# Gated cross-attention and feed-forward block, 8 batches on one core: the last batch in two halves of 112 queries, and a new order of all steps

## The reference, cut to what matters

```python
for b in range(8):                       # x: 8 x 224 x 512, ctx: 8 x 750 x 512, all float32
    q = layer_norm(layernorm(x[b])) * gq + betq ; c = layer_norm(ctx[b]) * gkv + betkv
    Q, K, V = q @ Wq + bq, c @ Wk + bk, c @ Wv + bv          # 16 heads of 32
    o = softmax(Q_h @ K_h.T / sqrt(32)) @ V_h                # per head: 224 x 750
    x1 = x[b] + tanh(g_x) * (concat_h(o) @ Wo + bo)
    h  = relu(layernorm(x1) @ ternary(W1).T + b1)            # 224 x 2048
    out[b] = x1 + tanh(g_f) * (h @ ternary(W2).T + b2)
```

## Time and profile before

| | us |
|---|---|
| median of 3 runs | 966.37 (963.3 to 967.71) |
| profiled execution, its own time | 963.93 |
| its span, first to last instruction | 962.1 |
| TensorE busy | 901.3 (94%) |
| VectorE busy | 745.5 (77%) |
| ScalarE busy | 641.4 (67%) |
| GpSimd busy | 298.2 (31%) |

### The profile page before, as it was taken

The page is one execution under the profiler, slowest core; times in us unless marked ns, Lnnn a source line. Parts: engine busy times, 40 slices in busy tenths (PEclk is TensorE's granted clock), DMA queues, the critical chain, the costliest instruction groups (busy, mean ns, idle before and its releaser), DMA issues.

```text
span 962.1 us, 22304 instructions
## 1 busy us (share of the span) xinstructions
PE 901.3 (94%) x8868; PEld 686.9 (71%) x8868; DVE 745.5 (77%) x1378; ACT 641.4 (67%) x1330; POOL 298.2 (31%) x517
## 2 busy tenths in 40 slices
...
GB/s 283 185 206 237 140 130 133 192 149 1 82 64 175 2 2 111 54 157 1 33 96 191 2 3 127 84 110 1 64 33 139 1 4 62 154 17 2 42 1 20
DMA packets 52039, 84.03 MB, mean 87 GB/s; under 512 B 6392, under 2 KB 33528, under 8 KB 50936
## 3 DMA queue, kind: packets, MB, share of 16 engines
...
## 4 chain that ended last, share of the span: by engine, by line
PE 78%; DVE 9%; DMA 5%; ACT 4%; SPq 3%; issue 1%; POOL 0%; DVEq 0%; ACTq 0%; POOLq 0%
PE ps_fill L481 49%; PE ps_pv L528 8%; PE ps_score L496 7%; PE ps_exp L512 7%; PE ps_fill L538 4%; DMA ctx_raw<-ctx_in 3%; DVE row_max L786 2%; SPq L401 2%; DVE p_parts L794 1%; PE ps_fill L586 1%; DVE bn L826 1%; DMA h_parts<-w2t 1%; ACT ps_exp L665 1%; ACT p_parts L664 1%; DVE h_parts L975 1%
## 5 line engine op out<-in xcount | busy, mean ns | idle before, releaser
L786 DVE TENSOR_REDUCE row_max<-ps_score 128x1 f32<-128x750 f32 x256 | 238.1, 930 | 34.7 <-PE ps_score L496 33.4
L794 DVE TENSOR_TENSOR p_parts<-ps_exp,p_parts 125x448 f16<-125x448 f32 x384 | 233.2, 617 | 33.8 <-ACT ps_exp L665 31.6
L664 ACT ACTIVATE p_parts<-ps_exp 125x448 f16<-125x448 f32 x384 | 209.1, 544 | 68.6 <-PE ps_exp L512 51.3
L665 ACT ACTIVATE ps_exp<-ps_exp 125x448 f32<-125x448 f32 x384 | 211.0, 549 | 0.0
L496 PE MATMUL ps_score<-k_stack,q_stack 96*128 96x375 f16 x512 | 128.1, 332 | 12.4 <-DVE row_max L786 11.9
L512 PE MATMUL ps_exp<-q_stack,k_stack 100*125 100x224 f16 x768 | 128.9, 267 | 7.3 <-DVE p_parts L794 5.6
L528 PE MATMUL ps_pv<-v_now,p_parts 125*128 125x66 f16 x3072 | 115.7, 194 | 2.8 <-DVE o_sum L802 1.3
L528 PEld LDWEIGHTS ps_pv<-v_now,p_parts 125*128 125x128 f16 x3072 | 109.3, 98 | 11.9 <-issue 3.5
L481 PE MATMUL ps_fill<-w_ternary,h_parts 128*128 128x256 fp8e4 x1024 | 116.6, 273 | 0.0
L512 PEld LDWEIGHTS ps_exp<-q_stack,k_stack 100*125 100x125 f16 x768 | 89.0, 139 | 29.0 <-DVE p_parts L794 6.9
L481 PEld LDWEIGHTS ps_fill<-w_ternary,h_parts 128*128 128x128 f16 x1024 | 99.4, 98 | 13.9 <-DVE ctx_t_lo L871 0.9
(11 more groups left out here) (139 smaller groups left out, 1550.5 us busy)
## 6 DMA issues: line engine op xcount, KB each, us to landing
...
```

The source lines that it names most:

```text
L664: nc.scalar.activation(ph[0:KR, unit, :], ps_exp[0:KR, u, 0:2 * NQ], ACT.Exp, scale=EXP_SCALE)
L665: nc.scalar.activation(ps_exp[0:KR, u, 0:2 * NQ], ps_exp[0:KR, u, 0:2 * NQ], ACT.Exp, scale=EXP_SCALE).then_inc(exp_done, 1)
L786: nc.vector.tensor_reduce(mx[:, i // 2, i % 2:i % 2 + 1], ps_score[:, :, 0:KH], AX.XY, ALU.max) \
L794: nc.vector.tensor_tensor(pl[0:KR, unit, :], ps_exp[0:KR, u, 0:2 * NQ], ph[0:KR, unit, :], ALU.subtract).then_inc(p_split, 1)
```

## The change

The attention and feed-forward of batch 7 are regrouped. `score`, `expo`, `pv`, `mr`, `split`, `f1` keep their number of steps, but a step of batch 7 now belongs to one half of 112 queries: scores 0 to 15 are the 16 heads of half 0, scores 16 to 31 those of half 1; `expo.3h` to `expo.3h+2` and `pv.h` take two heads of one half (h below 8: half 0); `f1.0` to `f1.3` are the 16 chunks of half 0, `f1.4` to `f1.7` those of half 1. An `expo` has four matmuls of 112 moving columns instead of two of 224, with the same 125 stationary columns each; a `pv` still has 24 matmuls of 66 moving columns, but 112 stationary ones instead of 128; an `f1` has 32 matmuls of 112 columns instead of 16 of 224, and ScalarE lifts it in four pieces of 112 instead of two of 224. `ot`, `op`, `yt`, `f2`, `score` work on 112 queries instead of 128. `divide`, `rstd2`, `bias2` and `store` of batch 7 become two steps, one per half, and their waits are per half. Nothing is computed twice or left out in either kernel.

Then the tail of half 0 up to `yt.0@7` is put in the list ahead of `pv.15@7`, and `f1.0@7` to `f1.3@7` right behind it, between the steps of half 1.

All three lists are new: they hold the same steps, but also in `OPENING` and `ROUND` nearly every step stands elsewhere. `OPENING` now reaches a little further, to `pv.15@1`. On SyncE's queue the end is now `kq.0@7 vc.0@7 vc.1@7 kq.1@7 kq.2@7 store.0@5 kq.3@7 vc.2@7 vc.3@7 xb.0@6 store.0@6 xb.0@7 store.0@7 store.1@7`.

After the change TensorE's queue ends `pv.11@7 f2.3@6 expo.39@7 pv.12@7 ot.0@7 expo.40@7 mr.7@7 expo.41@7 expo.42@7 expo.43@7 expo.44@7 pv.13@7 op.0@7 expo.45@7 expo.46@7 pv.14@7 expo.47@7 yt.0@7 pv.15@7 f1.0@7 f1.1@7 f1.2@7 ot.1@7 f1.3@7 op.1@7 f2.0@7 f2.1@7 yt.1@7 f1.4@7 f1.5@7 f1.6@7 f1.7@7 f2.2@7 f2.3@7`, and VectorE's `f2_add.3@6 max.31@7 part.39@7 part.40@7 ot_lo.0@7 part.41@7 part.42@7 take.12@7 part.43@7 part.44@7 take.13@7 op_add.0@7 rstd2.0@7 part.45@7 take.14@7 part.46@7 part.47@7 yt_lo.0@7 take.15@7 f1_hi.0@7 divide.1@7 ot_lo.1@7 f1_hi.1@7 f1_hi.2@7 f1_hi.3@7 op_add.1@7 rstd2.1@7 f2_add.0@7 f2_add.1@7 yt_lo.1@7 ...`.

```diff
@@ ENDING, last lines @@
-    f1_hi.7@6 pv.14@7 part.37@7 part.38@7 take.11@7 part.39@7 max.31@7 part.40@7 f2_add.0@6 take.12@7 f2.3@6
-    f2_add.1@6 part.41@7 take.13@7 part.42@7 split.7@7 part.43@7 pv.15@7 part.44@7 part.45@7 part.46@7 part.47@7
-    f2_add.2@6 f2_add.3@6 take.14@7 take.15@7 divide.0@7 bias.0@7 ot.0@7 ot.1@7 norm2.0@7 ot_lo.0@7 norm2.1@7 op.0@7
...
+    f2.3@6 max.28@7 take.9@7 f2_add.0@6 part.31@7 expo.39@7 pv.12@7 part.32@7 max.29@7 f2_add.1@6 part.33@7 max.30@7
+    part.34@7 part.35@7 take.10@7 divide.0@7 ot.0@7 expo.40@7 mr.7@7 expo.41@7 expo.42@7 part.36@7 part.37@7
+    take.11@7 expo.43@7 part.38@7 f2_add.2@6 expo.44@7 pv.13@7 f2_add.3@6 max.31@7 bias.0@7 op.0@7 part.39@7
+    part.40@7 ot_lo.0@7 part.41@7 part.42@7 take.12@7 part.43@7 part.44@7 take.13@7 expo.45@7 op_add.0@7 expo.46@7
+    pv.14@7 expo.47@7 norm2.0@7 yt.0@7 rstd2.0@7 part.45@7 take.14@7 part.46@7 part.47@7 pv.15@7 f1.0@7 yt_lo.0@7
+    take.15@7 f1_hi.0@7 divide.1@7 f1.1@7 f1.2@7 ot.1@7 ot_lo.1@7 f1_hi.1@7 f1.3@7 op.1@7 f2.0@7 norm2.1@7 f2.1@7
+    f1_hi.2@7 bias2.0@7 yt.1@7 f1.4@7 f1_hi.3@7 op_add.1@7 rstd2.1@7 f1.5@7 f1.6@7 f1.7@7 f2_add.0@7 f2_add.1@7
+    yt_lo.1@7 f1_hi.4@7 f1_hi.5@7 f1_hi.6@7 f2.2@7 f2.3@7 f1_hi.7@7 f2_add.2@7 bias2.1@7 store.1@7 f2_add.3@7
 
+        LAST = B - 1
+        HQ = NQ // 2
+
+        def half(t):
+
...
+                    if n == LAST:
+                        for t in range(2):
+                            sp.dma_start(xb[0:HQ, t, :], x[n][half(t), :]).then_inc(xb_loaded, 16)
+                    else:
+                        load_rows(n, xb, xb_loaded)
                 elif kind == "kq":
                     copy_kq(i, n)
                 elif kind == "vc":
                     copy_v(i, n)
+                elif kind == "store" and n == LAST:
+                    sp.wait_ge(out_ready, n * 4 + 2 * i + 2)
+                    sp.dma_start(out[n][half(i), :], xb[0:HQ, i, :]).then_inc(out_stored, 16)
                 elif kind == "store":
                     sp.wait_ge(out_ready, n * 4 + 4)
...
                     pe.wait_ge(kq_landed[h // 4], n * 96 + 96)
                 if n == 0 and i == 0:
                     pe.wait_ge(bias_row_ready, 3)
                 else:
                     pe.wait_ge(max_taken, n * 32 + i)
-                for half in range(2):
-                    last = pe.matmul(ps_score[:, half, 0:KH],
-                                     q_stack[0:SPLIT_ROWS, h, QSTART[t]:QSTART[t] + P],
-                                     k_stack[0:SPLIT_ROWS, h, half * KH:half * KH + KH],
-                                     start=True, stop=True)
+                q = half(t) if n == LAST else slice(QSTART[t], QSTART[t] + P)
+                for s in range(2):
+                    last = pe.matmul(ps_score[0:q.stop - q.start, s, 0:KH], q_stack[0:SPLIT_ROWS, h, q],
+                                     k_stack[0:SPLIT_ROWS, h, s * KH:s * KH + KH], start=True, stop=True)
                 last.then_inc(scores_ready, 1)
 
...
                     pe.wait_ge(p_split, n * 48 + (i - 2))
-                for kt in (2 * u, 2 * u + 1):
-                    last = pe.matmul(ps_exp[0:KR, u, (kt % 2) * NQ:(kt % 2) * NQ + NQ],
-                                     k_stack[0:STACK_ROWS, h, kt * KR:kt * KR + KR],
-                                     q_stack[0:STACK_ROWS, h, :], start=True, stop=True)
+                if n == LAST:
+                    for c in range(4 * u, 4 * u + 4):
+                        hc, kt = 2 * (h % 8) + c // KT, c % KT
+                        last = pe.matmul(ps_exp[0:KR, u, (c % 4) * HQ:(c % 4 + 1) * HQ],
+                                         k_stack[0:STACK_ROWS, hc, kt * KR:kt * KR + KR],
+                                         q_stack[0:STACK_ROWS, hc, half(h // 8)], start=True, stop=True)
+                else:
+                    for kt in (2 * u, 2 * u + 1):
+                        last = pe.matmul(ps_exp[0:KR, u, (kt % 2) * NQ:(kt % 2) * NQ + NQ],
+                                         k_stack[0:STACK_ROWS, h, kt * KR:kt * KR + KR],
+                                         q_stack[0:STACK_ROWS, h, :], start=True, stop=True)
                 last.then_inc(logits_ready, 1)
 
             def pv(h, n):
 
-                if h % 4 == 0:
+                if n == LAST:
+                    if h % 2 == 0:
+                        pe.wait_ge(v_landed[h % 8 // 2], n * 32 + 32)
+                elif h % 4 == 0:
                     pe.wait_ge(v_landed[h // 4], n * 32 + 32)
                 pe.wait_ge(p_split, n * 48 + (3 * h + 3))
                 if n * 16 + h >= 1:
                     pe.wait_ge(o_taken, n * 16 + h)
+                if n == LAST:
+                    for c in range(2 * KT):
+                        for part in (ph, pl):
+                            last = pe.matmul(
+                                ps_pv[0:HQ, c // KT * 2 * VW:(c // KT + 1) * 2 * VW],
+                                part[0:KR, 3 * (h % 2) + c // 4, (c % 4) * HQ:(c % 4 + 1) * HQ],
+                                v_now[0:KR, c % KT, 2 * (h % 8) + c // KT].rearrange("p a b -> p (a b)"),
+                                start=(c % KT == 0 and part is ph), stop=(c % KT == KT - 1 and part is pl))
+                    last.then_inc(pv_done, 1)
+                    return
                 for t in range(2):
                     for kt in range(KT):
...
                                  lambda a, c: whl["o"][a][:, c, :])
                 elif kind == "yt":
                     pe.wait_ge(y_normed, n * 2 + (i + 1))
-                    last = turn(P, bank, yo[:, i, :])
+                    rows = HQ if n == LAST else P
+                    last = turn(rows, bank, yo[:, i, :], rows)
                 elif kind == "f1":
+                    if n == LAST:
+                        if i % 4 == 0:
+                            pe.wait_ge(y_split, n * 2 + i // 4 + 1)
+                        for j in range(4):
+                            m = slice((i % 4 * 4 + j) * P, (i % 4 * 4 + j + 1) * P)
+                            last = three(ps_fill[:, bank, j * HQ:(j + 1) * HQ], lambda a, c: w1q[:, c, m],
+                                         lambda a, c: o_t[a][:, c, half(i // 4)], order=((0, 0), (0, 1)))
+                        last.then_inc(fill_ready, 1)
+                        return
                     if i == 0:
                         pe.wait_ge(y_split, n * 2 + 2)
...
 
-                        if c % 2 == 0:
+                        if n == LAST:
+                            if c % 4 == 0:
+                                pe.wait_ge(h_split, n * 8 + 2 * i + c // 4 + 1)
+                        elif c % 2 == 0:
                             pe.wait_ge(h_split, n * 8 + (c // 2 + 1))
                     t, w = i // 2, slice((i % 2) * 256, (i % 2 + 1) * 256)
-                    r = slice(QSTART[t], QSTART[t] + P)
-                    last = three(ps_fill[:, bank, 0:256], lambda a, c: (hh, hl)[a][:, c, r],
+                    r = half(t) if n == LAST else slice(QSTART[t], QSTART[t] + P)
+                    last = three(ps_fill[0:r.stop - r.start, bank, 0:256], lambda a, c: (hh, hl)[a][:, c, r],
                                  lambda a, c: w2q[:, c, w], order=((0, 0), (1, 0)), chunks=FC,
-                                 ready=ready if i == 0 else None)
+                                 ready=ready if i == 0 or (n == LAST and i == 2) else None)
                 last.then_inc(fill_ready, 1)
 
...
                 dve.wait_ge(scores_ready, n * 32 + (i + 1))
+                if n == LAST:
+                    h, t = i % H, i // H
+                    if i % 4 == 0:
+                        dve.wait_ge(max_split, (n - 1) * 8 + (h // 2 + 2))
+                    nc.vector.tensor_reduce(mx[0:HQ, h, t:t + 1], ps_score[0:HQ, :, 0:KH], AX.XY, ALU.max) \
+                        .then_inc(max_taken, 1)
+                    return
                 if i % 4 == 0 and n:
                     dve.wait_ge(max_split, (n - 1) * 8 + (i // 4 + 1))
...
+                                            ps_pv[0:HQ, 0:4 * VW].rearrange("p (h s d) -> p h d s", h=2, s=2),
+                                            AX.X, ALU.add).then_inc(o_taken, 1)
+                    return
                 nc.vector.tensor_reduce(o_sum[:, :, h, :],
                                         ps_pv[:, 0:4 * VW].rearrange("p (t s d) -> p t d s", t=2, s=2),
                                         AX.X, ALU.add).then_inc(o_taken, 1)
+
+            def divide_half(t, n):
+
+                dve.wait_ge(o_taken, n * 16 + 8 * t + 8)
+                nc.vector.reciprocal(rden[0:HQ, t, :], o_sum[0:HQ, t, :, HD]).then_inc(o_recip, 1)
+                dve.wait_ge(o_recip, n + (t + 1))
+                dve.wait_ge(y_split, n * 2)
+                nc.vector.tensor_tensor(yo[0:HQ, t, :].rearrange("p (h d) -> p h d", h=H),
+                                        o_sum[0:HQ, t, :, 0:HD],
```

(8 more changed lines are left out.)

366 lines of the change are left out of this document (219 added, 147 removed).

## The result

The changed kernel takes 973.98 us (median of 4 runs, 972.99 to 976.52), the kernel before 965.89 us (4 runs): ratio 1.009, 95% interval 1.0058 to 1.0121. It is slower; 958 was forecast, at most 968. The profiled execution took 972.99 us with a span of 971.2.

A forecast was written before the change was run, and what follows sets the result against it. TensorE was taken to bound the rounds and, after the change, batch 7's attention. Tail -14.6, attention +6.4, rounds and opening 0 gave -8.2 us: 955.7 profiled, median 958, 8-in-10 range 946 to 968.

The forecast's parts named there:

- part 1: Tail behind `pv.15@7`: overlapping the halves takes it from 53.1 to 38.5 us, minus 14.6.
- the sum without clock: Tail behind `pv.15@7`: its steps added at full clock, 36.3 us, before 2.2 was added for the clock.
- parts 2 and 3: Last `pv` of batch 6 to that of 7: moved steps add 4.3 us to TensorE, narrower loads 7.7 and 1.9.
- the sum by pieces: Last `pv` of batch 6 to that of 7, kernel before: TensorE's work at full clock, one piece per kind, 64.8 us.
- Waiting: of 10.5 us much was VectorE's, which now has more cover ... 6.5 in all: Last `pv` of batch 6 to that of 7: TensorE's waits go from 10.5 to 6.5 us, 3 of them new.
- Half clock: 6.0 before, the cause of most of it gone: 2.5: Last `pv` of batch 6 to that of 7: half-clock cost, laid to the wait for batch 7's V, falls to 2.5 us.
- 0 to 1 us: At `score.12@7`: wait for the copies of `kq.3@7` behind `store.0@5`, 0 to 1 us, counted within the waiting.
- Part 4: New order of the rest: rounds minus 0.9 and plus 0.9 us; opening 0, with 4 us either way.
- Minus 0.9 and plus 0.9: Rounds: the long one may lose its 0.9 us, and a possible new TensorE wait in each adds 0.9.
- the rounds pay: Rival: K, Q or V copies asked for too late at each batch change, 3.7 to 10 us, so 966; chance 0.13.
- 4 more: Last `pv` of batch 6 to that of 7: 4 us above the forecast 87.7 if waits stay at 10.5.
- dearer loads: Rival: narrow loads hold TensorE's array as long as `expo`'s pace allows, plus 13.7 us, so 980; chance 0.08.

The follow-up runs named there:

- warm_end: Changed kernel plus 64 idle matmuls, results overwritten, where TensorE waited near the start and end of batch 7's attention; 967.94 us, 1.0000 to 1.0041 against the kernel before.
- wide_pv: Changed kernel with `pv` of batch 7 loading 128 columns of p again instead of 112; 966.86 us, 0.9963 to 1.0012 against the kernel before.
- narrow_all: Kernel before with every `pv` product except the first head's loading 112 columns of p instead of 128; 1026.33 us, 1.0563 to 1.0624 against the kernel before.
- full_new_lists: Kernel before, full tiles and its own tail, with the changed kernel's `OPENING` and `ROUND`; 972.11 us, 1.0013 to 1.0062 against the kernel before.
- kq_first: Changed kernel with batch 7's last key and value copies ahead of batch 5's store on SyncE; 973.68 us, 1.0035 to 1.0094 against the kernel before.
- warm_keys: Changed kernel with 64 idle matmuls where TensorE waited and batch 7's last key and value copies ahead of batch 5's store; 968.91 us, 1.0017 to 1.0066 against before.
- early_half: Changed kernel with half 0's steps up to `yt.0` between `pv.9` and `pv.13`, its residual in a free buffer, batch 6's f2 between last heads; 971.62 us.

## Why the prediction was wrong

- **The tail (part 1): right.** 38.5 forecast, 37.9 measured; in warm_end, at the full clock, 35.9 against the 36.3 of the sum without clock. The gap at `yt.1` is there, the clock is 1 from a few us on. The 15 us are the halves' overlap, of which some 2 are clock.
- **TensorE's work in the stretch (parts 2 and 3): the total right, in part by luck.** Loads of 112 columns at 133 ns, `pv` 1.22 (1.2 forecast), `expo` 0.22 to 0.25 (0.23); in all 79.0 us against 78.7. But the windows have TensorE busy 74.00 us in the kernel before, so 74.0 - 6.0 = 68.0 at the full clock where the sum by pieces had 64.8, and the halves added 79.0 - 68.0 = 11.0 and not 13.9. The two errors cancel. wide_pv and narrow_all show that the width of the loads alone costs 7 to 8 us; without it the changed kernel would be level with the one before (0.9963 to 1.0012).
- **The failed step: "Waiting: of 10.5 us much was VectorE's, which now has more cover ... 6.5 in all" and "Half clock: 6.0 before, the cause of most of it gone: 2.5".** The waits were 12.5 and the half clock 7.4, together 10.9 us more than the 9.0 put down. Four things were wrong in it. The base: 10.5 was the remainder of a sum that was 3.2 us short, and TensorE stood idle 81.30 - 74.00 = 7.3 us before; so the waits rose by 5.2 and did not fall by 4.0. The cause: V was not what the half clock came from. It is granted from 829.2 on the earlier trace rows, and ahead of that TensorE had waited for VectorE, while the wait for V ended at 836.5 and cost it 0.3 us. From the timeline of the kernel before:

```profile
826.83 0.90 PE L528 MATMUL ps_pv<-v_now,p_parts 125*128 125x66 f16 x24 [0.69 <-DVE p_parts L794]
...
829.25 0.81 PE L496 MATMUL ps_score<-k_stack,q_stack 96*128 96x375 f16 x2 [1.08 <-DVE row_max L786]
```

The cover: more work on TensorE did not hide VectorE's maxima, the scores waited 4.2 us for them instead of 2.8, and at the start of the stretch the divide (0.9) and the keys of heads 12 to 15 (1.0, at the edge of the "0 to 1 us" forecast) joined them. At the end f2 of batch 6 had been used up before `pv.12`, so that TensorE waited 2.7 us from 914 to 919, mostly on work of ScalarE and VectorE, a gap that the prediction didn't have. The clock: behind each of these spots stands a stretch of half clock, which the prediction counted for one old wait only. The wait at `op_add.0` and `yt.0` was forecast (3 us; 2.7 at `yt.0`, 3.5 of VectorE at `op_add.0`).
- **Part 4, the rounds: the term was mis-sized.** "Minus 0.9 and plus 0.9" was +2.3, and batch 6 +2.0. The rival "the rounds pay" has its sign and the size of its low end, but not its mechanism: no copy is late (idle 0.2 us in a round), TensorE's order itself costs more. Of batch 6, by the starts of TensorE's instructions, 1.1 us lie at `expo`, with 108 matmuls instead of 94, those of the halved batch among them, and 1.0 at `pv`. full_new_lists, without halves, has the same 1.0 at `pv`, is 2.5 us longer there in all and 1.2 shorter in the stretch, so the list alone can do it, and what in it stays open. The 2.0 us of opening and batch 1 are not explained; those two together took 299 to 304 us in the profiled executions of the other versions (narrow_all, which is slower everywhere, apart), 299.4 in before.
- **The range** ended at 968 because waits of 10.5 us counted as the bad case ("4 more"), and because half clock was not given a range of its own. With 12.5 and 7.4 the same sum gives 98.6 us for the stretch. The chance of a slower kernel, 0.14, was there for dearer loads, rounds or the opening; no rival had more waiting in the stretch.

That the half clock comes from TensorE's idle time, and that it costs 7.4 us in the stretch, is shown by warm_end; the 12.5 us of waiting are read from the trace. That taking away one wait of several that end close together brings nothing is shown by kq_first and warm_keys. That the cover was spent too early is the reading of the windows and of early_half, whose gain was mostly eaten by the clock; it is less firmly shown.
